# Edge lists in runs of 112 and 13 partitions, chunk firsts by a strided view, features in fourteen pieces behind them: the preparation of a two-layer graph network kernel

## The reference, cut to what matters

```python
h = jnp.maximum(_layernorm(x, axis=-1), 0.0)
x = x + _L0_gnn_ref(h, edge_index, edge_weight, L0_gnn_W1_w, L0_gnn_W1_b)   # gathers by src, sums by dst, degrees
h = jnp.maximum(_layernorm(x, axis=-1), 0.0)
x = x + _L1_gnn_ref(h, src, dst, ...)      # two layers: h @ W_self.T + mean over neighbours @ W_neigh.T + b
```

## Time and profile before

| | |
|---|---|
| Time, median of 3 runs | 4103.68 us (4092.16 to 4107.59) |
| The profiled execution's own time | 4083.7 us |
| its span | 4082.0 us |
| PE, DVE, ACT, POOL busy | 90%, 49%, 29%, 70% |
| Mean granted TensorE clock | 0.989 |

### The profile page before, as it was taken

How to read it: one execution, slowest core, us unless ns; L and a number is a source line. 1 busy time by engine, 2 the same in 40 slices (tenths; PEclk the granted TensorE clock), 3 DMA queues, 4 the chain that set the end, 5 groups by cost and what they waited for, 6 DMA issues and landing times.

```text
span 4082.0 us, 67151 instructions
## 1 busy us (share of the span) xinstructions
PE 3657.9 (90%) x24852; PEld 2338.9 (57%) x24852; DVE 2011.0 (49%) x5255; ACT 1180.2 (29%) x3014; POOL 2848.1 (70%) x2859
## 2 busy tenths in 40 slices
PE   0028999999999999998999999999999999999998
PEld 0015666666666666665666665556555656666555
DVE  3579999977777777772233233232321113121211
ACT  0043466666666666661022021121200001000000
POOL 5603877777777777754777777777747777777775
PEclk9998999999999999999999999999999999999999
DMA  5171466666666666558776776766787776777775
GB/s 158 46 181 65 160 216 194 205 208 218 203 220 197 221 200 217 197 190 272 255 252 216 294 252 222 280 238 236 268 277 257 284 253 232 275 273 270 274 267 207
DMA packets 384251, 913.33 MB, mean 224 GB/s; under 512 B 74159, under 2 KB 318088, under 8 KB 363186
## 3 DMA queue, kind: packets, MB, share of 16 engines
q1 hardware_dynamic: 194385, 603.47, 40.0%
q0 software_dynamic: 132000, 274.23, 22.3%
q10 hardware_dynamic: 57536, 31.25, 2.8%
HBM read 664.23 MB, written 245.39 MB: 223 GB/s over the span
## 4 chain that ended last, share of the span: by engine, by line
PE 40%; POOL 36%; issue 12%; DVE 7%; DMA 4%; ACT 1%; DVEq 0%; POOLq 0%; ACTq 0%; SPq 0%
POOL arena L1255 33%; PE ps L1460 30%; PE ps L1373 5%; PE ps L1431 3%; DMA arena<-parts,arena 3%; DVE arena L1685 2%; DVE arena L1682 2%; POOL arena L1220 2%; PE ps L1408 2%; DMA arena<-in_dst 1%; DMA table<-arena 1%; PE ps L1398 0%; ACT arena L1130 0%; POOL arena L1245 0%; POOL arena L1230 0%
## 5 line engine op out<-in xcount | busy, mean ns | idle before, releaser
L1255 POOL DMA_INDIRECT arena<-parts,arena x2643 | 2683.6, 1015 | 950.1 <-issue 790.5
L1460 PE MATMUL ps<-arena 128*128 128x384 bf16 (+1 forms) x15974 | 3054.3, 327 | 19.1 <-DVEq L1759 11.2
L1460 PEld LDWEIGHTS ps<-arena 128*128 128x128 bf16 x15974 | 1544.1, 98 | 931.9 <-ACT arena L1051 21.8
L1051 ACT ACTIVATE arena<-ps 128x392 bf16<-128x392 f32 x1824 | 903.0, 497 | 1007.5 <-PE ps L1431 994.5
L1431 PE MATMUL ps<-arena 128*128 128x196 bf16 (+1 forms) x5102 | 1034.8, 238 | 103.4 <-DVE arena L1685 96.0
L1710 DVE TENSOR_TENSOR arena<-arena 128x640 bf16<-128x640 bf16 (+1 forms) x577 | 261.0, 462 | 1188.0 <-PE ps L1373 1186.9
L1431 PEld LDWEIGHTS ps<-arena 128*128 128x128 bf16 x5102 | 479.2, 101 | 321.4 <-DVE arena L1685 96.9
L1682 DVE TENSOR_TENSOR arena<-arena 128x768 bf16<-128x768 bf16 (+3 forms) x881 | 475.6, 540 | 247.3 <-PE ps L1431 242.6
L1373 PE MATMUL ps<-arena 128*128 128x384 bf16 (+1 forms) x2643 | 532.7, 330 | 63.2 <-DMA arena<-parts,arena 62.8
L1685 DVE TENSOR_TENSOR arena<-arena 128x1176 bf16<-128x1176 bf16 (+4 forms) x881 | 555.9, 631 | 0.0
L1373 PEld LDWEIGHTS ps<-arena 128*128 128x128 bf16 x2643 | 254.4, 98 | 228.0 <-issue 76.3
(11 more groups left out here) (155 smaller groups left out, 1177.3 us busy)
## 6 DMA issues: line engine op xcount, KB each, us to landing
arena<-counts SPq DMA_DIRECT2D x102, 3136.0 KB
counts<-arena SPq DMA_DIRECT2D x56, 3136.0 KB
arena<-parts,arena POOLq DMA_INDIRECT x2643
arena<-parts SPq DMA_DIRECT2D x28, 672.0 KB, 9.6
arena<-table SPq DMA_DIRECT2D x196, 64.0 KB
parts<-arena ACTq DMA_DIRECT2D x109, 96.0 KB
parts<-arena SPq DMA_DIRECT2D x14, 679.0 KB, 7.1
parts<-arena SPq DMA_DIRECT2D x87, 96.0 KB
```

Of the source, the lines that this page charges most:

```text
L1051: act.activation(stage[k][:, :, a - g * P:b - g * P], ps[:, unit_bank(q), 0:(b - a) * tiles].rearrange("p (n a) -> p a n", n=b - a), ACT.C ...
L1255: pool.indirect_dma_start(ring[:, m % RSUBS * CHUNKS + c, 0:W0 if nth == 0 else W1C], None, parts_of[nth], bass.IndirectOffsetOnAxis(ap=ta ...
L1460: m = pe.matmul(bank(b, 0, w), stage[k][:, a, :], Xp[:, a, 0:w], start=e == 0, stop=e == tiles - 1, skip_group_check=True)
```

## The change

1. The load of the chunks' first words goes, with its tile and semaphore. DVE reads the same words from dst itself by a view with a step of 128 words, and waits for all four loads of dst.
2. dst, src and the store of `rec` are each cut into a transfer of the first 112 partitions (`WHOLE`) and one of the rest: 12 for dst, whose last partition had loads of its own already, and 13 for src and `rec`.
3. ACT waits for dst, and then issues X in 14 loads of seven tiles, each with a semaphore of its own (`s_xp[n]`, counted on by one load in later passes). DVE waits for X group by group.
4. The room block stands ahead of the gathers on POOL.

```diff
-        first_i, first_li, first_hi = (part(SLOTS, dt=I32) for _ in range(3))
+        first_li, first_hi = (part(SLOTS, dt=I32) for _ in range(2))
+        WHOLE = iters // 16 * 16
...
         @block.sync
-                sp.dma_start(first_i[0:iters, :], dst.rearrange("(i k e) -> i k e", k=SLOTS, e=P)[:, :, 0]).then_inc(s_first, 16)
-                sp.dma_start(dst_i[0:iters - 1, :], bass.AP(dst.tensor, 0, [[STEP, iters - 1], [1, STEP + 1]])).then_inc(s_dst, 16)
+                for a, b in ((0, WHOLE), (WHOLE, iters - 1)):
+                    sp.dma_start(dst_i[a:b, :], bass.AP(dst.tensor, a * STEP, [[STEP, b - a], [1, STEP + 1]])).then_inc(s_dst, 16)
...
-                sp.dma_start(src_i, src.rearrange("(i e) -> i e", e=STEP)).then_inc(s_src, 16)
+                for a, b in ((0, WHOLE), (WHOLE, iters)):
+                    sp.dma_start(src_i[a:b, :], src[a * STEP:b * STEP].rearrange("(i e) -> i e", e=STEP)).then_inc(s_src, 16)
...
-            sp.dma_start(records[0:n_edges, :].rearrange("(i e) k -> i e k", e=STEP), rec).then_inc(s_recd, 16)
+            for a, b in ((0, WHOLE), (WHOLE, iters)):
+                sp.dma_start(records[a * STEP:b * STEP, :].rearrange("(i e) k -> i e k", e=STEP), rec[a:b]).then_inc(s_recd, 16)
...
-            sp.wait_ge(s_recd, 32)
+            sp.wait_ge(s_recd, 48)
...
         @block.scalar
-            for i in range(loops):
-                t = 2 * HALF * i
-                act.dma_start(X[:, t:t + 2 * HALF, :], x[t * P:(t + 2 * HALF) * P, :].rearrange("(t p) f -> p t f", p=P)).then_inc(s_x, 16)
+            act.wait_ge(s_dst, 4 * 16)
+            for n in range(halves):
+                t = n * HALF
+                act.dma_start(X[:, t:t + HALF, :], x[t * P:(t + HALF) * P, :].rearrange("(t p) f -> p t f", p=P)).then_inc(s_xp[n], 16)
...
         @block.gpsimd
+            done = 0
+            for k, (a, n, vs) in enumerate(batches):
+                pool.memset(room[:, k:k + 1], float(P * vs[0])).then_inc(s_room, 1)
...
             pool.wait_ge(s_prepared_dve, 3)
             for t in range(tiles):
...
-                if t == 20:
-                    done = 0
-                    for k, (a, n, vs) in enumerate(batches):
...
-                pool.wait_ge(s_recd, 32)
+                pool.wait_ge(s_recd, 48)
...
         @block.tensor
-                    pe.wait_ge(s_xp[a // HALF], 16 * nth)
+                    pe.wait_ge(s_xp[a // HALF], 16 * nth + 16)
...
         @block.vector
-            dve.wait_ge(s_first, 16)
+            dve.wait_ge(s_dst, 4 * 16)
             dve.wait_ge(s_iden, 1)
-            dve.tensor_scalar(first_li[0:iters, :], first_i[0:iters, :], P - 1, None, ALU.bitwise_and)
-            own(dve.tensor_scalar(first_hi[0:iters, :], first_i[0:iters, :], 7, None, ALU.arith_shift_right))
+            firsts = dst_i[:, 0:STEP].rearrange("i (k e) -> i k e", e=P)[:, :, 0]
+            dve.tensor_scalar(first_li[0:iters, :], firsts, P - 1, None, ALU.bitwise_and)
+            own(dve.tensor_scalar(first_hi[0:iters, :], firsts, 7, None, ALU.arith_shift_right))
...
-            dve.wait_ge(s_dst, 3 * 16)
...
-            dve.wait_ge(s_src, 16)
+            dve.wait_ge(s_src, 2 * 16)
...
                 count_near(q)
-                if q == 0:
-                    dve.wait_ge(s_x, loops * 16)
+                dve.wait_ge(s_xp[q], 16)
                 statistics(q)
```

More of the change, by code:

```diff
@@ L406, in program @@
         s_const = sem("s_const")
-        s_first = sem("s_first")
         s_dst = sem("s_dst")
@@ L410, in program @@
         s_w = sem("s_w")
-        s_x = sem("s_x")
         s_own = sem("s_own")
@@ L856, in _ @@
         def _(sp):
-            with nc.allow_non_contiguous_dma(reason="single words and runs of five"):
-                sp.dma_start(first_i[0:iters, :], dst.rearrange("(i k e) -> i k e", k=SLOTS, e=P)[:, :, 0]).then_inc(s_first, 16)
-                sp.dma_start(dst_i[0:iters - 1, :], bass.AP(dst.tensor, 0, [[STEP, iters - 1], [1, STEP + 1]])).then_inc(s_dst, 16)
+            with nc.allow_non_contiguous_dma(reason="single words"):
+                for a, b in ((0, WHOLE), (WHOLE, iters - 1)):
+                    sp.dma_start(dst_i[a:b, :], bass.AP(dst.tensor, a * STEP, [[STEP, b - a], [1, STEP + 1]])).then_inc(s_dst, 16)
                 sp.dma_start(dst_i[iters - 1:iters, 0:STEP], dst[n_edges - STEP:n_edges].rearrange("(i e) -> i e", i=1)).then_inc(s_dst, 16)
                 sp.dma_start(dst_i[iters - 1:iters, STEP:STEP + 1], dst[n_edges - 1:n_edges].rearrange("(i e) -> i e", i=1)).then_inc(s_dst, 16)
-                sp.dma_start(src_i, src.rearrange("(i e) -> i e", e=STEP)).then_inc(s_src, 16)
+                for a, b in ((0, WHOLE), (WHOLE, iters)):
+                    sp.dma_start(src_i[a:b, :], src[a * STEP:b * STEP].rearrange("(i e) -> i e", e=STEP)).then_inc(s_src, 16)
             for k, w in enumerate((W1, Wn0, Ws0, Wn1, Ws1)):
@@ L1213, in _ @@
             pool.memset(eps_c[:, :], EPS).then_inc(s_const, 1)
+            done = 0
+            for k, (a, n, vs) in enumerate(batches):
+                pool.memset(room[:, k:k + 1], float(P * vs[0])).then_inc(s_room, 1)
+                done += 1
+                for i in range(1, len(vs)):
+                    if vs[i] != vs[i - 1]:
+                        pool.wait_ge(s_room, done)
+                        pool.affine_select(out=room[:, k:k + 1], in_=room[:, k:k + 1], compare_op=ALU.is_gt, fill=float(P * vs[i]),
+                                           base=i, pattern=[[0, 1]], channel_multiplier=-1).then_inc(s_room, 1)
+                        done += 1
+            pool.memset(tail_room, float(P * tail_visits[0])).then_inc(s_room, 1)
+            done += 1
+            for i in range(1, tails):
+                if tail_visits[i] != tail_visits[i - 1]:
+                    pool.wait_ge(s_room, done)
+                    pool.affine_select(out=tail_room, in_=tail_room, compare_op=ALU.is_gt, fill=float(P * tail_visits[i]),
+                                       base=i, pattern=[[0, 1]], channel_multiplier=-1).then_inc(s_room, 1)
+                    done += 1
             pool.wait_ge(s_prepared_dve, 3)
```

## The result

The changed kernel takes 4080.02 us (median of 5 runs, 4073.14 to 4082.95) against 4103.68 of before; the ratio is 0.9938, with a 95% interval of 0.9913 to 0.9963. That is 23.7 us less, and clear of no change. The forecast was 4079.7.

A forecast was written before the change was run, and what follows sets the result against it. Preparation was taken as bound by a dependence chain through the last gather's start. Profiled 4083.7 us minus 24 gave 4059.7, plus the 20.0 offset 4079.7 us; own range 4070 to 4089, overall 4064 to 4098.

The forecast's parts named there:

- What bounds: Preparation before the main part: a microsecond off the last gather's start is one off the end, unless something else becomes later.
- The landing of dst: Load of dst at the start: 1.6 MB over 16 engines with X held back, landing between 7 and 11 us.
- rival (b): Load of dst: 112 partitions still run on five engines, dst lands at 27.9, gain 10.5 us, time 4093.2; chance 0.10.
- DVE's start: DVE's first instruction: starts at 10.9 us instead of 26.1, with iota_w its other wait and dst hidden or just not.
- POOL's holds: POOL beside DVE: affine_selects and gathers held; constants end at 18.7 or 17.4 for the last held one, gather 0 29.2, gather 4 40.0.
- Rival (a): POOL's preparation: DVE's holds don't bite, no gather is stopped, last gather 37 us earlier, time 4066.7; chance 0.08.
- The gathers behind: Gathers after gather 4: 93 steps of 1.248 us plus 1 us, so gather 97 starts at 157.1.
- stray holds: Later gathers: 1 us in all, as DVE has no backlog and counts each group as it lands; 2.7 before.
- X behind dst: ACT's 14 loads of X after dst: 6.4 MB, 25 us at 256 GB/s, some 45 with others beside, hidden from DVE.
- The offset: Step from profiled execution to timed median: 20.0 us, taken over from the kernel before, giving 4079.7 from 4059.7.
- the 24 us: Last gather's start in the preparation: 157.1 against 181.48, 24.4 us earlier, taken as 24.

The follow-up runs named there:

- the second profile: The changed kernel and the kernel before, each profiled again unaltered: ratio 0.9944 for the changed kernel, 0.9999 for the kernel before.
- the uncut side: The changed kernel with the cut undone, dst in 124 partitions and one, src and the store in 125; ratio to before 0.9963.
- five of the variants: Five unlisted ones among the follow-up kernels that edit the kernel before or the changed one; the follow-up kernels' ratios to before run from 0.9922 to 0.9996.

## Why the prediction was right, point by point

**What bounds.** That a microsecond off the last gather is one off the end held: 22.6 us of preparation, 23.7 of time. The stretch from the last gather to the first landing stayed what it was, 23.7 us before and 23.4 after.

**The landing of dst.** I put 7 to 11 us; it was 11.1 at most in the first profile and 11.37 in the second, at the far end or past it. The engines were all at work between 5 and 10 us, but gave 1.06 MB, 13 GB/s each, where I had taken 18.6 to 26.6 from rows with five engines at work. What the working left out is that dst wasn't alone. By 11.1 us the queue had moved 2.28 MB, and dst is 1.6 of them; src and the weights took the rest. From first bytes at some 1.9 us that is 248 GB/s, close to the 256 that I took from X, and dst alone would by it have landed at about 8.4 (an estimate). The row, 0 to 11.1 us of the changed kernel:

```profile
q1 hardware_dynamic: 209, 2.28, 85.0%
```

The rule of the Trainium skill (DMA: Bandwidth & Descriptors, Why a DMA increments its semaphore by 16 and not by 1) is that the number of engines is the largest divisor up to 16. The trace agrees roughly on the uncut side, where transfers for which it has 4 and 5 engines took 35.9% of 16, which is 5.7, and fully on the cut one, 100.6%. The Trainium skill's rule against splitting (same page, Rules for kernel authors), cited for rival (b), gives as its reason that either part fills all 16 engines; the uncut transfer here used a third of them, so the reason didn't apply, and the cut was worth 12.6 us or more.

**DVE's start.** 10.9 forecast, 11.19 measured, by `iota_w` as I said. That was close to chance: dst was there 0.1 us sooner at least, and in the second profile, where `iota_w` was made by 10.36, dst released DVE at 11.37.

**POOL's holds.** The step on which the sum rested most. Constants freed at 17.96 (15.22 + 2.74) against 17.4; gather 0 at 29.68 against 29.2; gather 4 at 40.74 against 40.0. Rival (a) is out: a tensor_tensor did stop gathers, 4.25 us for the first in five of the variants. The Trainium skill's page SBUF — State Buffer, section Who interferes with whom, infers that a tensor_tensor doesn't stop descriptor generation. It also says there that a DVE instruction with two inputs in SBUF contends with a GpSimd instruction that reads SBUF. The gather reads its indices there, and the 4.25 us against 0.94 agree with this second statement, which the prediction passed over; whether descriptors are made meanwhile, no row tells.

**The gathers behind.** 116.3 us for the 93 steps from gather 4, and 2.2 us of stray holds where I had put 1: last start 159.2 against 157.1. I had said that DVE counts each group as it lands. It doesn't at first: gathers took up to 10.9 us to land (2.5 in the median), DVE waited 14.5 us for the first seven until 54.14, and then worked off a backlog beside gathers. The records' store is the likely cause, as it moved 1.54 MB between 40 and 45 us and as much in the next five, with X beside it at first; no run takes it away. This term was mis-sized, and is 1.2 of the 2.1 us by which the last gather came later than forecast; most of the rest is gather 4.

**X behind dst.** Hidden, as forecast: none of DVE's waits up to the flag is for X. But I argued that X had filled the engines and that its waiting helped dst. The run without the wait shows that it doesn't: this sentence of the prediction was wrong, at no cost to the sum.

**The offset.** The sum came to 4059.7 by the profiled execution, and its successor took 4082.95. Only the step to the median, 20.0 us, which I took over without a reason for its size, met the result. The first profile of before was 8.5 us faster than the fastest of the five timed runs; its part behind the flag was 23 us shorter than that of the second profile. The forecast of 4079.7 thus owes its closeness partly to a difference of medians, which it was right to use, and to luck in the scatter; the 24 us are what was predicted.

## What to carry to other kernels

- Read an edit's price where it will stand, not where it stood: moving the same room block was worth 8 to 11 us or 5 to 7, the same cut 0.5 to 3 or 13 to 15, as other waits covered them. Parts of a change that each move a start don't add.
- When DVE works beside POOL's indirect loads, count the instructions that hold it, not DVE's time: each of the long ones here held one gather until it ended, be it with two inputs (3.49 us) or, like L1573, with one (1.83 us). The reductions didn't (3.49 us).
- Where an edit is worth 0.5% and the main part scatters by as much, compare the milestone in the trace (here the first landing) as well as the medians, and never two spans.

## What the runs showed of the hardware

- Loads in packets of 12.8 KB gave 1.06 and 1.22 MB in 5 us with all engines at work (5 to 10 and 10 to 15 us of the changed kernel), and 1.10 and 1.33 in its second profile: 212 to 267 GB/s. X, in packets of 512 bytes, gave 1.46 MB in 5 us on its own queue, 292 GB/s. I had expected the longer packets to be no slower; why they are stays open. The row for X, from 25 to 30 us of the changed kernel:

```profile
q10 hardware_dynamic: 2909, 1.46, 115.8%
```

- dst, in its long packets, lost little to X's short ones on the same engines: it landed at 11.17 and 12.04 with X beside it, at 11.0 to 11.5 without. Up to 11.17 us the queue of dst and src had moved 2.15 MB and that of X 0.13.
- Memsets on POOL pass a DVE instruction with two inputs, as far as the rows show: 21 took 0.76 us, the end of it beside L1582, and 0.91 us in the changed kernel beside DVE's short instructions. Affine_selects and gathers don't pass one, nor the tensor_scalar of 1.83 us with one input.
- The load of 3125 single words took 25.3 us to land, and the issue behind it on the same queue took 19.16 us. Without it the four issues of dst are through by 2.3 us.
